# A hybrid network on one core: the selective-scan layers with another split of their work over the engines

## The chip, the cores and the metric

The kernel runs on one core of a Trainium2 chip. A core has five engines with instruction queues of their own: TensorE (PE, matrix products into PSUM), VectorE (DVE), ScalarE (ACT), GpSimd (POOL) and SyncE (SP, which here issues the DMAs). They meet only at semaphores. The metric is the device time of one execution in microseconds; lower is better.

## The reference, cut to what matters

The network takes x of shape (2, 16, 16, 64): two batches of 256 positions with 64 channels. It runs an edge-attention block, a rope attention, a wide attention, a mixture of experts, six selective-scan (mamba) layers and a last mixture of experts. Only the six layers, and what is loaded for them, are changed:

```python
# for each of the 6 layers, on h of shape (2, 256, 64); dI = 128, DS = 16 states, rank 16
r = h * rsqrt(mean(h * h, -1) + eps) * norm_w
u, z = split(r @ in_w, 2)                      # 128 channels each
uc = silu(causal_conv(u, cw, 4 taps) + cb)
dt_r, Bm, Cm = split(uc @ xp_w, (16, 16, 16))
dt = softplus(dt_r @ dt_w + dt_b)
# scan over the 256 positions, for each channel and each of the 16 states:
#   s[t] = exp(dt[t] * A) * s[t-1] + dt[t] * uc[t] * Bm[t];   y[t] = sum over states of s[t] * Cm[t]
h = h + ((y + uc * D) * silu(z)) @ out_w
```

## The kernel before, in words

A layer runs as two units, one for each batch, so there are 12 units (`UNITS`). A unit holds its 128 channels on the partitions and its 256 positions on the columns. The 16 states are done in four groups of four (`NSG`, `SG`), each group one tile of 128x1024. For each group the kernel needs a decay tile (`da`, four exponentials on ACT, L1405), a drive tile (`dbu`, dt times uc times B), one scan on DVE (L1133, 128x1024), the product of the states with C (`hc`), and the sum over states, which TensorE does by adding the four slices of `hc` into PSUM with four products by the identity matrix (`sum_y`, L664).

B and C are 16 rows each, and must stand on all 128 partitions. That is done in two ways. The f32 rows go to DRAM (`spill`) and come back broadcast (groups 1 to 3 of B and group 1 of C). Or the rows are split in three bf16 parts, stacked on 96 partitions (`stack`), and TensorE spreads one row at a time with a column of picks (`spread_b` L634, `spread_c` L643). DVE takes the tiles that TensorE spread (drive of group 0 at L1121, C products of groups 0, 2 and 3 at L1140). POOL takes those that came by DMA (drives of groups 1 to 3 at L1611, C product of group 1 at L1619).

While a unit is scanned, the next one is prepared: squares and mean on ACT and POOL, two transposes (`prep_transpose`), the input products with the convolution folded in (`prep_in`), tanh on ACT, `prep_uc` on DVE (L1078), the product that gives B, C and the rank-16 rows (`prep_x`, L623), the product for dt (`prep_dt` on PE, L627), and softplus as a polynomial in four quadratics (ACT L1391, POOL, DVE L1098 and L1102). After the last sum of a unit, DVE multiplies it by the gate (`gate`, L1085), TensorE projects it out (L672) and DVE adds it to the residual (L1089).

The order on each engine is written out by hand: `pe_step`, `v_step`, `a_step` and `p_step`, with eight units inside a loop of two turns. An engine works strictly in that order. In `pe_step` three products that nobody reads stand behind the first spread of C (`keep_awake`, L655). Weights come layer by layer into two tiles (`wmt`).

What an instruction of the loop waits for is a count of a semaphore: `m_y` is raised by the last sum of a unit, `m_gate` by the gate, `m_h` by each scan, `m_uc`, `m_xds`, `m_dt` by the pieces named so.

Of the kernel before, what the change touches and what calls it, by code (L numbers as in the profile page):

```python
# [13 lines left out]
F32 = mybir.dt.float32  # L14
# [5 lines left out]
P = 128  # L20
# [56 lines left out]
def hybrid(nc, x, const, w0, w1, w2, w3, w5, wm, rows, out):  # L77
    ctx = ExitStack()
    with ctx:
# [3 lines left out]
        spill = nc.dram_tensor("spill", (B, DS + SG, N), F32, kind="Internal").ap()  # L83
# [12 lines left out]
        wmt = [sb(f"wmt{k}", [P, WM.size]) for k in range(2)]  # L96
# [14 lines left out]
        pick_b = sb("pick_b", [P, 32], BF16)  # L111
# [88 lines left out]
        xds, stack = two("xds", [P, N]), two("stack", [P, N], BF16)  # L200
        rest = sb("rest", [64, N])
        wcv, alog, amat = two("wcv", [P, 2 * P]), two("alog", [P, DS]), two("amat", [P, DS])
        dmat = two("dmat", [P, P])
# [1554 lines left out]
```

## Time and profile before

| | us |
|---|---|
| median of 3 runs | 411.38 |
| the three runs | 409.92, 411.38, 411.42 |
| span of the profiled execution | 409.9 |
| the lowest run, the nearest to that span | 409.92 |
| busy: PE 340.5, DVE 314.7, ACT 249.1, POOL 210.6 | |
| first gate (unit 0) to last gate (unit 11) | 178.5 to 379.7 |

Busy shares are 83% for PE, 77% for DVE, 61% for ACT and 51% for POOL, over stages with different limits. The 12 units take the span from about 145 to 380 us. A row of the chain of waits is a piece of the work that ended last, followed back; a row of a timeline has start, duration, engine and line, operation, tiles written and read, the count of instructions merged in it, and in brackets the idle time ahead of it with who ended it. An f32 product is two instructions of TensorE, so "x24" at L664 is twelve products.

### The profile page before, as it was taken

Reading aid. Unit: us, or ns where it says so; the run is one execution under the profiler, and the core shown is the slowest. Engines: PE = TensorE matmul, PEld = TensorE weight load, DVE = VectorE, ACT = ScalarE, POOL = GpSimd, SP = SyncE. Lnnn points to the kernel's source line nnn. Section 1 sums busy time; section 2 is a strip of 40 time slices with the busy share of each in tenths; the row PEclk is TensorE's granted clock in tenths of the full one; section 3 lists DMA queues with packets and bytes.
Section 4 is the critical chain, followed back from the end, with each engine's and each line's share of the span. In section 5 each row is a group of like instructions: output and inputs, shape, how many; then the busy total and the mean of one; then the engine's idle time right before and its main releaser. Section 6 shows DMA issues by size and latency. Waiting matters only on the chain.

```text
span 409.9 us, 5884 instructions
## 1 busy us (share of the span) xinstructions
PE 340.5 (83%) x1818; PEld 235.1 (57%) x1818; DVE 314.7 (77%) x538; ACT 249.1 (61%) x681; POOL 210.6 (51%) x235
## 2 busy tenths in 40 slices
PE   5868998999899986888887979888888879768674
PEld 3356765565584654566664757566566647557442
DVE  2674678898653618779999799979988999998653
ACT  2012378888727455948778586948676786862170
POOL 1985000000000028788889698868977797882000
PEclk9985999999979997899999899899989999987868
DMA  7900000000002105142450515161342326050000
GB/s 238 403 7 1 2 1 2 0 2 2 0 2 64 40 4 206 44 165 75 173 178 31 208 43 205 29 220 62 144 162 86 123 86 210 3 203 0 2 0 13
DMA packets 11345, 35.24 MB, mean 86 GB/s; under 512 B 2368, under 2 KB 2992, under 8 KB 11192
## 3 DMA queue, kind: packets, MB, share of 16 engines
q1 hardware_dynamic: 11032, 34.61, 23.9%
q10 hardware_dynamic: 288, 0.33, 0.3%
q8 instruction: 12, 0.20, 0.2%
q14 instruction: 13, 0.11, 0.1%
HBM read 34.54 MB, written 0.39 MB: 85 GB/s over the span
## 4 chain that ended last, share of the span: by engine, by line
PE 53%; DVE 24%; ACT 12%; issue 5%; DMA 3%; POOL 2%; DVEq 0%; SPq 0%; POOLq 0%; ACTq 0%
PE PS L664 15%; DVE big L1133 7%; ACT PS L1405 4%; PE PS L511 4%; PE PS L643 3%; DVE big L1121 3%; DVE big L1140 3%; PE PS L475 2%; ACT sg L1368 2%; PE PS L289 2%; PE PS L295 2%; PE PS L627 2%; PE PS L405 2%; PE PS L575 2%; PE PS L485 2%
## 5 line engine op out<-in xcount | busy, mean ns | idle before, releaser
L1133 DVE TENSOR_TENSOR_SCAN big<-PS,big 128x1024 f32<-128x1024 f32 x48 | 109.3, 2284 | 3.0 <-ACT PS L1405 2.7
L664 PE MATMUL PS<-big,cst 128*128 128x256 f32 x384 | 96.0, 407 | 0.0
L1405 ACT ACTIVATE PS<-dt,amat 128x255 f32<-128x255 f32 x192 | 80.1, 466 | 25.4 <-DVE dt L1105 21.5
L1611 POOL TENSOR_TENSOR big<-dtu,big 128x1024 f32<-128x1024 f32 x36 | 84.2, 2356 | 7.2 <-DVE dtu L1108 6.6
L664 PEld LDWEIGHTS PS<-big,cst 128*128 128x128 f32 x384 | 76.8, 205 | 14.9 <-issue 3.7
L1644 POOL TENSOR_SCALAR lnv<-mv 128x4 f32<-128x4 f32 x1 | 0.4, 418 | 93.9 <-DVE mv L770 93.9
L1140 DVE TENSOR_TENSOR big<-big,PS 128x1024 f32<-128x1024 f32 x36 | 43.8, 1216 | 0.9
L1239 ACT ACTIVATE big<-PS 128x512 f32<-128x512 f32 (+1 forms) x43 | 24.8, 584 | 22.3 <-PE PS L511 7.3
L643 PE MATMUL PS<-stack,pick_b 96*128 96x256 bf16 x144 | 23.9, 292 | 17.0 <-DVE big L1140 9.2
L1286 ACT ACTIVATE big<-PS,big 128x256 f32<-128x256 f32 x64 | 29.8, 475 | 1.5 <-DVE big L902 1.5
L1619 POOL TENSOR_TENSOR big<-big 128x1024 f32<-128x1024 f32 x12 | 28.3, 2358 | 1.1 <-DVE big L1133 1.1
L643 PEld LDWEIGHTS PS<-stack,pick_b 96*128 96x128 bf16 x144 | 11.8, 102 | 27.0 <-DVE big L1140 12.5
L902 DVE TENSOR_REDUCE big<-PS 128x2 f32<-128x512 f32 x32 | 22.0, 688 | 6.5 <-PE PS L405 3.1
L655 PE MATMUL PS<-cst 128*128 128x256 f32 x102 | 26.2, 396 | 0.0
L511 PE MATMUL PS<-cst,big 128*128 128x128 f32 x128 | 20.9, 285 | 3.2 <-ACT big L1239 1.9
L1597 POOL TENSOR_TENSOR big<-big,quad_t 128x256 f32<-128x256 f32 x24 | 14.2, 612 | 15.5 <-ACT big L1391 15.5
L511 PEld LDWEIGHTS PS<-cst,big 128*128 128x128 f32 x128 | 13.5, 140 | 14.4 <-DVE big L911 6.9
L655 PEld LDWEIGHTS PS<-cst 128*128 128x128 f32 x102 | 19.0, 198 | 3.0 <-issue 0.7
L911 DVE TENSOR_SCALAR big<-big 128x256 f32<-128x256 f32 x64 | 19.7, 350 | 1.1
L1391 ACT ACTIVATE big<-PS,quad_t 128x256 f32<-128x256 f32 x48 | 18.9, 477 | 0.4
L295 PE MATMUL PS<-cst 128*128 128x256 f32 x62 | 18.7, 436 | 0.0
L1361 ACT ACTIVATE ht<-PS,wmt 64x256 f32<-64x256 f32 x24 | 11.3, 471 | 12.1 <-PE PS L609 11.8
(309 smaller groups left out, 624.6 us busy)
## 6 DMA issues: line engine op xcount, KB each, us to landing
big<-spill SPq DMA_DIRECT2D x48, 512.0 KB, 5.6
wmt<-in_wm SPq DMA_DIRECT2D x6, 418.0 KB, 3.2
w3t<-in_w SPq DMA_DIRECT2D x1, 1588.0 KB, 13.5
big<-routed SPq DMA_DIRECT2D x8, 128.0 KB, 3.0
w2t<-in_w SPq DMA_DIRECT2D x1, 896.0 KB, 10.1
cst<-in_const SPq DMA_DIRECT2D x1, 848.0 KB, 8.0
w5t<-in_w SPq DMA_DIRECT2D x1, 812.0 KB, 15.0
w1t<-in_w SPq DMA_DIRECT2D x1, 385.0 KB, 8.4
```

What stands on the lines that cost most here:

```text
L295: pe.matmul(PS[:, bank, N:2 * N], ident, CONST.of(cst, "rope")[:, 0:N], start=True, stop=True)
L511: last = pe.transpose(PS[:, 6 + t, m * N + a * P:m * N + (a + 1) * P], probs[:, i % SLOTS, a, m * P:(m + 1) * P], ident)
L643: last = pe.matmul(PS[:, 4 + c, s * N:(s + 1) * N], pick_b[0:96, col:col + 1].to_broadcast([96, P]), stack[b][0:96], start=True, stop=True)
L655: pe.matmul(idle_ps, ident, CONST.of(cst, "rope")[:, 0:N], start=True, stop=True)
L664: last = pe.matmul(yps, ident, hc[:, g, s], start=False, stop=(g == NSG - 1 and s == SG - 1))
L1133: v.tensor_tensor_scan(flat(hst[g][:]), flat(da[g % 2]), flat(dbu[:, g]), 0.0, ALU.mult, ALU.add).then_inc(sem("m_h"), 1)
L1140: v.tensor_tensor(hc[:, g], hst[g][:], BCv, ALU.mult).then_inc(sem("m_hc"), 1)
L1239: copy = lambda dst, src, **kw: act.activation(dst, src, ACT.Copy, **kw)
L1286: act.activation(probs[:, i % SLOTS, a], PS[:, i % 4, a * N:(a + 1) * N], ACT.Exp, bias=rowmax[:, i, a:a + 1], accum_out=rowsum[:, i, a:a ...
L1405: one = act.activation(da[g % 2][:, n, 1:N], dt[b][:, 1:N], ACT.Exp, scale=amat[k][:, col:col + 1])
L1611: pool.tensor_tensor(dbu[:, g], dtu[b][:].unsqueeze(1).to_broadcast([P, SG, N]), bsp[b][:, SG * (g - 1):SG * g], ALU.mult).then_inc(sem("m ...
L1619: pool.tensor_tensor(hc[:, 1], hst[1][:], csp[b][:], ALU.mult).then_inc(sem("m_hc_pool"), 1)
```

## The change

The arithmetic is the same network in another split:

- All weights of the six layers are loaded at the start (`wr`, `wxd`, `wout`, `cols`, `inz`, `wcv`, `winu`), and the rank-16 weight is multiplied into one 128x128 weight for dt (`wdt`), by transposes and products placed in the first attention stage. The loop over units is straight code for all 12.
- The biases of the convolution and of dt are rows of ones times a bf16 stack (`bias`), one more product each in `prep_in` and `prep_x`.
- The three bf16 parts of B and C are made inside PSUM: `prep_x` writes three copies of the rows (times two), ACT takes the first part out, TensorE subtracts it from the other two (`split_hi`), ACT takes the second out, TensorE subtracts it (`split_mid`), ACT takes the third.
- DVE now drives groups 0 and 1 and multiplies C only for group 3 (`weigh_last`, in two halves). POOL drives groups 2 and 3 and multiplies C for groups 0, 1 and 2. C of groups 0 to 2 and B of groups 2 and 3 come by DMA: five broadcasts of 512 KB a unit in place of four.
- The normed rows are written twice by ACT (`prep_hs`) in place of once by POOL. The residual is a product by the identity that starts the sum of the output projection, and ACT copies it back.
- Softplus is another formula: Abs, Exp, Tanh and three Squares on ACT, then two fused operations on DVE; POOL has no part in it.
- `keep_awake` stands only ahead of unit 0. `prep_uc` moves on DVE from behind scan 2 to behind scan 1. On TensorE the sums of group 0 move behind `prep_x` and `split_hi`.

```diff
--- before.py
+++ after.py
+            def prep_in(u):
+
+                i, b = divmod(u, 2)
+                pe.wait_ge(sem("m_ht"), u + 1)
+                pe.matmul(ups, bias[:, i, :, 0], ones[:], start=True, stop=False)
+                pe.matmul(ups, wcv[:, i, 0], ht[b][:, 3:3 + N], start=False, stop=False)
+                pe.matmul(ups, wcv[:, i, 1], ht[b][:, 1:1 + N], start=False, stop=True).then_inc(sem("m_in"), 1)
+                pe.matmul(zps, inz[:, i], ht[b][0:64, 3:3 + N], start=True, stop=True).then_inc(sem("m_in"), 1)
...
+                pe.matmul(dtp, bias[:, i, :, 1], ones[:], start=True, stop=False)
+                pe.matmul(dtp, wdt[:, i], uc[b], start=False, stop=True)
+                pe.matmul(xd[64:96], wxd[:, i, 0:32], uc[b], start=True, stop=True).then_inc(sem("m_xd"), 1)
+                pe.matmul(xd[0:64], wxd[:, i, 0:64], uc[b], start=True, stop=False).then_inc(sem("m_xd"), 1)
+
+            def split_hi(u):
+
+                pe.wait_ge(sem("m_xs"), 4 * u + 2)
+                pe.wait_ge(sem("m_sp"), 6 * u + 1)
+                pe.matmul(xd[0:32], less_hi[64:96], stack[u % 2][64:96], start=False, stop=False)
+                pe.matmul(xd[32:64], less_hi[64:96], stack[u % 2][64:96], start=False, stop=True).then_inc(sem("m_less"), 1)
+
+            def split_mid(u):
+
+                pe.wait_ge(sem("m_xs"), 4 * u + 3)
+                pe.matmul(xd[0:32], less_mid[32:64], stack[u % 2][32:64], start=False, stop=True).then_inc(sem("m_less"), 1)
...
+            def out_proj(u):
+
+                i, b = divmod(u, 2)
+                if u + 1 < UNITS:
+                    pe.wait_ge(sem("m_dt"), u + 2)
+                if u >= 2:
+                    pe.wait_ge(sem("m_ycp"), u - 1)
+                pe.matmul(hidp, ident, Y[:, :, b], start=True, stop=False)
                 pe.wait_ge(sem("m_gate"), u + 1)
                 for a in range(HALF):
-                    last = pe.matmul(hidp[:, a], yg[b][:, a * P:(a + 1) * P], WM.of(wmt[k], "out"),
-                                     start=True, stop=True)
...
-                if not first:
-                    sum_y(u + -1, nb, NSG - 1)
-                spread_b(u, b)
-                if not first:
-                    out_proj(u + -1, pk, nb)
-                pe.wait_ge(sem("m_dbu0"), u + 1)
-                spread_c(u, b, 0)
-                if not last:
-                    keep_awake(3)
-                sum_skip(u, k, b)
-                if not last:
-                    prep_transpose(u + 1, nk, nb)
-                pe.wait_ge(sem("m_hc"), u * 3 + 1)
-                spread_c(u, b, 2)
-                if not last:
-                    prep_in(u + 1, nk, nb, i * 2 + (s + 1) // 2 + 1)
-                sum_y(u, b, 0)
-                if not last:
-                    prep_x(u + 1, nk, nb)
-                if not last:
-                    prep_dt(u + 1, nk, nb)
-                pe.wait_ge(sem("m_hc"), u * 3 + 2)
-                spread_c(u, b, 3)
-                sum_y(u, b, 2)
-                sum_y(u, b, 1)
...
+            for u in range(UNITS):
+                more = u + 1 < UNITS
+                if u:
+                    sum_y(u - 1, 2)
+                    sum_last(u - 1)
+                spread_first(u)
+                if u:
+                    out_proj(u - 1)
+                spread_second(u)
+                if more:
+                    prep_transpose(u + 1)
+                    prep_in(u + 1)
+                spread_last(u)
+                if more:
+                    prep_x(u + 1)
+                sum_skip(u, u + 1 if more else None)
+                if more:
+                    split_hi(u + 1)
+                sum_y(u, 0)
+                if more:
+                    split_mid(u + 1)
+                sum_y(u, 1)
+            sum_y(UNITS - 1, 2)
+            sum_last(UNITS - 1)
...
+            for u in range(UNITS):
+                prep_dt(u)
+                if u:
+                    gate(u - 1)
+                drive(u, 0)
+                scan(u, 0)
+                drive(u, 1)
+                scan(u, 1)
+                if u + 1 < UNITS:
+                    prep_uc(u + 1)
+                scan(u, 2)
+                scan(u, 3)
+                weigh_last(u)
             scaled = hs2[0][:].rearrange("p a (b e) -> p a b e", b=B)
...
+            def prep_xd(u):
+
+                act.wait_ge(sem("m_xd"), 2 * u + 2)
+                act.activation(xds[u % 2][:], xd[64:96], ACT.Copy, scale=0.5).then_inc(sem("m_xs"), 1)
+                act.activation(stack[u % 2][64:96], xd[64:96], ACT.Copy, scale=0.5).then_inc(sem("m_xs"), 1)
+
+            def prep_softplus(u):
+
+                act.activation(sp_a, dtp, ACT.Abs).then_inc(sem("m_sp"), 1)
+                act.wait_ge(sem("m_sp"), 6 * u + 1)
+                act.activation(sp_u, sp_a, ACT.Exp, scale=-1.0).then_inc(sem("m_sp"), 1)
+                act.activation(sp_v, sp_a, ACT.Tanh, scale=0.5, bias=turn_t).then_inc(sem("m_sp"), 1)
+                act.wait_ge(sem("m_less"), 2 * u + 1)
+                act.activation(stack[u % 2][32:64], xd[32:64], ACT.Copy, scale=0.5).then_inc(sem("m_xs"), 1)
+                act.wait_ge(sem("m_sp"), 6 * u + 3)
+                act.activation(sp_3, sp_u, ACT.Square, bias=a2_t).then_inc(sem("m_sp"), 1)
+                act.activation(sp_1, sp_v, ACT.Square, bias=a_t).then_inc(sem("m_sp"), 1)
+                act.wait_ge(sem("m_less"), 2 * u + 2)
+                act.activation(stack[u % 2][0:32], xd[0:32], ACT.Copy, scale=0.5).then_inc(sem("m_xs"), 1)
+                act.wait_ge(sem("m_sp"), 6 * u + 5)
+                act.activation(sp_2, sp_1, ACT.Square, scale=LOG_ROOT, bias=b_t).then_inc(sem("m_sp"), 1)
+
...
+            for u in range(UNITS):
+                more = u + 1 < UNITS
+                drive(u, 2)
+                if more:
+                    prep_rms(u + 1)
+                drive(u, 3)
+                for g in range(3):
+                    weigh(u, g)
+                if more:
+                    prep_gz(u + 1)
 
...
```

Engine TensorE, the second half of a unit, from the product on the fresh uc to the first spread of the next unit. Before (L623 is `prep_x`, L627 `prep_dt`, L643 the spread of C for group 3, L664 the sums, L634 the spread of B):

```order
L664 MATMUL PS<-big,cst 128x256 x4
L623 MATMUL PS<-uc,wmt 112x256
L627 MATMUL PS<-xds,wmt 128x256
L643 MATMUL PS<-stack,pick_b 128x256 x4
L664 MATMUL PS<-big,cst 128x256 x12
L634 MATMUL PS<-stack,pick_b 128x256 x4
```

Now (L637 to L640 are `prep_x`, L685 `sum_skip`, L646 and L647 `split_hi`, L652 `split_mid`, L691 and L698 the sums, L659 the spread):

```order
L637 MATMUL PS<-ones,bias 128x256
L638 MATMUL PS<-unit_t,wdt 128x256
L639 MATMUL PS<-unit_t,wxd 32x256
L640 MATMUL PS<-unit_t,wxd 64x256
L685 MATMUL PS<-unit_t,w0t 128x256
L646 MATMUL PS<-stack,less_hi 32x256
L647 MATMUL PS<-stack,less_hi 32x256
L691 MATMUL PS<-big,cst 128x256 x4
L652 MATMUL PS<-stack,less_mid 32x256
L691 MATMUL PS<-big,cst 128x256 x8
L698 MATMUL PS<-big,cst 128x256 x4
L659 MATMUL PS<-stack,pick_b 128x256 x4
```

The four sums of group 0, which stood ahead of `prep_x`, now stand behind it and behind `split_hi`; all 16 sums follow in one piece.

Engine TensorE, the first half of a unit, from the output projection to `prep_x`. Before (L655 is `keep_awake`):

```order
L672 MATMUL PS<-wmt,yg 128x64 x2
L643 MATMUL PS<-stack,pick_b 128x256 x4
L655 MATMUL PS<-cst 128x256 x3
L650 MATMUL PS<-uc,dmat 128x256
L609 MATMUL PS<-cst,hs 128x128 x2
L643 MATMUL PS<-stack,pick_b 128x256 x4
L615 MATMUL PS<-ht,wcv 128x256
L616 MATMUL PS<-ht,wcv 128x256
L617 MATMUL PS<-ht,wmt 128x256
L664 MATMUL PS<-big,cst 128x256 x4
```

Now:

```order
L708 MATMUL PS<-Y,cst 128x128
L711 MATMUL PS<-wout,unit_t 128x64 x2
L659 MATMUL PS<-stack,pick_b 128x256 x4
L621 MATMUL PS<-cst,hs 128x128 x2
L628 MATMUL PS<-ones,bias 128x256
L629 MATMUL PS<-ht,w2t 128x256
L630 MATMUL PS<-ht,w2t 128x256
L631 MATMUL PS<-ht,inz 128x256
L659 MATMUL PS<-stack,pick_b 128x256 x4
```

The three idle products, the skip product and four sums have gone from this stretch; small bias and identity products have come.

Engine DVE, one unit from its gate on. Before (L1121 drive, L1133 scan, L1140 C product, L1078 uc, L1098 and L1102 the polynomial):

```order
L1085 TENSOR_TENSOR yg<-PS,gz 128x256
L1121 TENSOR_TENSOR big<-dtu,PS 128x1024
L1089 TENSOR_TENSOR Y<-Y,PS 128x2x64
L1133 SCALAR_TENSOR_TENSOR big<-PS,big 128x1024
L1140 TENSOR_TENSOR big<-big,PS 128x1024
L1133 SCALAR_TENSOR_TENSOR big<-PS,big 128x1024 x2
L1078 SCALAR_TENSOR_TENSOR uc<-PS,wmt,sg 128x256
L1140 TENSOR_TENSOR big<-big,PS 128x1024
L1133 SCALAR_TENSOR_TENSOR big<-PS,big 128x1024
L1140 TENSOR_TENSOR big<-big,PS 128x1024
L1098 SCALAR_TENSOR_TENSOR PS<-big,PS 128x256 x2
```

Now (L1130 gate, L1137 drive, L1146 scan, L1110 uc, L1156 C product, L1116 and L1119 the polynomial):

```order
L1130 TENSOR_TENSOR unit_t<-PS,unit_t 128x256
L1137 TENSOR_TENSOR big<-unit_t,PS 128x1024
L1146 SCALAR_TENSOR_TENSOR big<-PS,big 128x1024
L1137 TENSOR_TENSOR big<-unit_t,PS 128x1024
L1146 SCALAR_TENSOR_TENSOR big<-PS,big 128x1024
L1110 SCALAR_TENSOR_TENSOR unit_t<-unit_t,PS 128x256
L1146 SCALAR_TENSOR_TENSOR big<-PS,big 128x1024 x2
L1156 TENSOR_TENSOR big<-big,PS 128x512 x2
L1116 SCALAR_TENSOR_TENSOR big<-big 128x256
L1119 SCALAR_TENSOR_TENSOR big<-big 128x256
```

Between the gate and uc there stand two drives and two scans, where there were one drive, three scans and one C product.

## Rows read from the trace of the kernel before

**Rows 1.** Page: the chain by engine, and the broadcasts (count, size, us to landing).

```profile
PE 53%; DVE 24%; ACT 12%; issue 5%; DMA 3%; POOL 2%; DVEq 0%; SPq 0%; POOLq 0%; ACTq 0%
...
big<-spill SPq DMA_DIRECT2D x48, 512.0 KB, 5.6
```

**Rows 2.** Stretches, two neighbouring units: us, busy (instructions) by engine, PE clock, DMA.

```profile
271.60:289.40 17.80, 15.06 (x72) 10.93 (x72) 17.32 (x17) 13.33 (x38) 13.96 (x17) 1.00 0.34 118
289.40:309.00 19.60, 16.95 (x72) 12.11 (x72) 16.80 (x16) 13.75 (x38) 16.93 (x14) 0.91 0.35 132
```

**Rows 3.** Chain of waits in those units: start us, us, what.

```profile
283.71 5.18 PE PS L664 x24
288.89 0.45 PE PS L634 x4
289.37 1.22 DVE big L1121
290.71 2.30 DVE big L1133
...
301.73 6.80 PE PS L664 x24
```

**Rows 4.** Timeline of DVE, same unit; columns as told under time and profile.

```profile
285.96 0.89 DVE L1098 SCALAR_TENSOR_TENSOR PS<-big,PS 128x256 f32<-128x256 f32 x2
287.48 0.42 DVE L1105 TENSOR_TENSOR dt<-PS,sp_m 128x256 f32<-128x256 f32 x1
288.93 0.42 DVE L1085 TENSOR_TENSOR yg<-PS,gz 128x256 f32<-128x256 f32 x1
293.04 1.22 DVE L1140 TENSOR_TENSOR big<-big,PS 128x1024 f32<-128x1024 f32 x1
294.17 4.67 DVE L1133 TENSOR_TENSOR_SCAN big<-PS,big 128x1024 f32<-128x1024 f32 x2
298.75 0.46 DVE L1078 SCALAR_TENSOR_TENSOR uc<-PS,wmt,sg 128x256 f32<-128x256 f32 x1
```

**Rows 5.** Timeline of PE: prep_x.

```profile
299.27 0.69 PE L623 MATMUL PS<-uc,wmt 128*112 128x256 f32 x2 [0.65 <-DVE uc L1078]
```

**Rows 6.** Timeline of ACT behind the decays of group 3.

```profile
300.00 0.38 ACT L1377 ACTIVATE xds<-PS 112x256 f32<-112x256 f32 x1
300.41 0.42 ACT L1379 ACTIVATE stack<-xds 96x256 bf16<-96x256 f32 x1
301.16 0.45 ACT L1385 ACTIVATE PS<-PS,wmt 128x256 f32<-128x256 f32 x1 [0.34 <-PE PS L627]
```

**Rows 7.** Timeline of POOL: one drive.

```profile
289.35 2.35 POOL L1611 TENSOR_TENSOR big<-dtu,big 128x1024 f32<-128x1024 f32 x1
```

**Rows 8.** Stretches inside unit 289.4 to 309.0, and one of the last unit.

```profile
290.70:296.60 5.90, 4.99 (x24) 3.17 (x24) 5.77 (x5) 4.77 (x14) 5.74 (x6) 1.00 0.01 3
296.60:301.40 4.80, 3.68 (x17) 2.31 (x17) 4.80 (x4) 4.26 (x12) 4.80 (x4) 1.00 0.02 4
301.50:304.80 3.30, 3.30 (x10) 2.65 (x9) 3.11 (x4) 2.64 (x8) 1.92 (x4) 0.50 0.55 174
366.40:373.10 6.70, 4.45 (x12) 3.00 (x12) 6.63 (x5) 4.36 (x9) 5.35 (x3) 0.50 0.00 0
```

**Rows 9.** Timeline of unit 0: ACT and DVE.

```profile
149.78 0.48 DVE L1078 SCALAR_TENSOR_TENSOR uc<-PS,wmt,sg 128x256 f32<-128x256 f32 x1 [4.32 <-ACT zs L1371]
152.21 0.45 ACT L1385 ACTIVATE PS<-PS,wmt 128x256 f32<-128x256 f32 x1 [0.34 <-PE PS L627]
156.50 0.42 DVE L1105 TENSOR_TENSOR dt<-PS,sp_m 128x256 f32<-128x256 f32 x1
```

**Rows 10.** Timeline of DVE: gates of units 0, 10 and 11.

```profile
178.47 0.42 DVE L1085 TENSOR_TENSOR yg<-PS,gz 128x256 f32<-128x256 f32 x1 [1.70 <-PE PS L664]
...
362.85 0.42 DVE L1085 TENSOR_TENSOR yg<-PS,gz 128x256 f32<-128x256 f32 x1 [0.55 <-PE PS L664]
...
379.74 0.42 DVE L1085 TENSOR_TENSOR yg<-PS,gz 128x256 f32<-128x256 f32 x1 [1.77 <-issue]
```

More of the change, by code:

```diff
@@ L198, in hybrid @@
+        uc, gz, dt, dtu, yg, tu, zs, zt = ([unit_t[:, N * (2 * n + t):N * (2 * n + t + 1)] for t in range(2)]
+                                           for n in range(8))
         ht = two("ht", [P, N + 4])
         hs2 = two("hs2", [P, HALF, P])
[L200 to L203, printed above, removed]
+        xds, stack = two("xds", [32, N]), two("stack", [96, N], BF16)
@@ L708, in _, with keep_awake @@
-            keep_awake(7)
-            prep_transpose(0, 0, 0)
+            def keep_awake(count, bank=5):
+                for _ in range(count):
+                    pe.matmul(PS[:, bank, N:2 * N], ident, CONST.of(cst, "rope")[:, 0:N], start=True, stop=True)
+            keep_awake(7, 6)
+            prep_transpose(0)
             keep_awake(1)
-            prep_in(0, 0, 0, 1)
-            keep_awake(4)
-            prep_x(0, 0, 0)
+            pe.wait_ge(sem("m_weights"), 5)
+            prep_in(0)
@@ L714, in _ @@
+            keep_awake(3)
+            prep_x(0)
             keep_awake(1)
-            prep_dt(0, 0, 0)
+            split_hi(0)
+            keep_awake(1)
+            split_mid(0)
             keep_awake(5)
-            pe_step(0, 0, first=True)
-            with pe.Fori(0, 2) as i:
-                for s in range(1, 5):
-                    pe_step(i, s)
-            for s in range(9, 12):
-                pe_step(0, s, last=(s == 11))
-            sum_y(UNITS - 1, 1, NSG - 1)
-            out_proj(UNITS - 1, 1, 1)
+            for u in range(UNITS):
[20 more added lines that the diff above has]
+                sum_y(u, 1)
@@ L1142, in _, with drive @@
-            prep_uc(0, 0, 0)
-            v_step(0, 0, first=True)
-            with v.Fori(0, 2) as i:
-                for s in range(1, 5):
-                    v_step(i, s)
-            for s in range(9, 12):
-                v_step(0, s, last=(s == 11))
+                v.tensor_tensor(yg[u % 2], yps, gz[u % 2], ALU.mult).then_inc(sem("m_gate"), 1)
+            def drive(u, g):
+                v.wait_ge(sem("m_BC"), 3 * u + g + 1)
+                if g == 0:
+                    v.wait_ge(sem("m_dtu"), u + 1)
+                v.tensor_tensor(dbu[:, g], dtu[u % 2].unsqueeze(1).to_broadcast([P, SG, N]), BCv, ALU.mult)\
+                    .then_inc(sem("m_dbu"), 1)
```

626 lines of the change are left out of this document (284 added, 342 removed).

## The prediction

> **What bounds the kernel now.** I read the page's chain first: TensorE holds 53% of what ended last and DVE 24% [rows 1]. Then I cut the 12 units into stretches. They come in two lengths, 17.8 us with the PE clock at its upper level (1.00, 2.4 GHz) and 19.6 us with a mean of 0.91 [rows 2]. In the short unit DVE is busy for 17.32 us of 17.8, and yet the chain does not stay on it: it runs over the twelve sums on PE, 5.18 us (0.43 each), the spread of B, the first drive and the scan [rows 3]. So two cycles are nearly equal, the work of DVE and a loop that goes through DVE, PE and ACT. In the long unit the same twelve sums take 6.80 us [rows 3], because the clock is at 0.50 (1.2 GHz) from 301.5 to 304.8 [rows 8], and 1.62 us arrive at the gate. A change gains only if it shortens both cycles.
>
> **DVE, part by part.** From one gate to the next it will do: gate 0.44 (288.93 to 289.37), two drives with their handover at 1.34 (289.37 to 290.71) [rows 3, 4], four scans at 2.3, uc 0.46, the last C product in two halves, about 1.25 (one was 1.22), and four small operations at 0.46 where five stood [rows 4]. That is 0.44 + 2.68 + 9.2 + 0.46 + 1.25 + 1.84 = 15.9 us in place of 17.3. By DVE alone a unit would fall from a mean of 18.4 ((362.85 - 178.47) / 10 [rows 10]) to about 16.2.
>
> **POOL and DMA.** POOL does five tiles of 2.35 us [rows 7] and small work of under 2 us, 13.5 us a unit. The drives are ready before their scans and the C products before their sums, except at the very end (below). Five broadcasts replace four; each lands in about 5.6 us [rows 1], and the first is wanted about 5 us after the rows leave ACT. If it is late by a microsecond the delay goes into POOL's wait for the squares of the next unit. Cost taken: nothing; without that cover, up to 1 us a unit.
>
> **The loop through PE, which I expect to decide.** The new order puts all sixteen sums behind prep_x and split_hi, and these behind uc. I follow it from the start of a gate:
> - Gate 0.44, first drive 1.34, scan 0 until the next operation 2.33 (290.71 to 293.04), second drive 1.34, scan 1 2.29 (half of 294.17 to 298.75): 7.74 us to uc [rows 3, 4].
> - uc to the first product behind it: 0.52 (298.75 to 299.27) [rows 4, 5].
> - prep_x was one f32 product, 0.69 with its tail. It gets two more at 0.43 and a bf16 one at 0.11 (four bf16 spreads took 0.45 [rows 3]): 1.66, and 0.04 to ACT. 1.70.
> - ACT copies the rows twice, 0.41 and 0.38 between starts, and takes Abs, 0.45 [rows 6], with 0.04 for the handover: 1.28. The skip product (0.43) lies beside this.
> - split_hi 0.22, sixteen sums 6.91, split_mid 0.11 between the first four and the rest, some 0.15 for three small weights: 7.4 us, and the next gate starts.
>
> The sum is 7.74 + 0.52 + 1.70 + 1.28 + 7.4 = 18.6 us at full clock. The same steps for the kernel before (0.44, 1.34, 2.33, 1.13, 4.58, 0.52, 0.73, 0.43, 0.63, 0.54, 5.22) give 17.9 where 17.8 was measured, so the method is good to a few tenths. DVE will be done 2.4 us before the last sum and wait at its gate. What was won by moving uc ahead of a scan (2.3 us) goes back through four more sums behind uc (1.7) and two more products in prep_x (1.0).
>
> ACT's work hides: two more small copies and no sigmoid copy for u; from Abs to the last Square six operations of about 0.4 and a wait for split_mid, some 3.5 us. They end about 4 us ahead of the last sum.
>
> **The clock.** Between gate and uc, 7.7 us, PE now has the projection (0.9 with the identity product), two spreads (1.2), two transposes (0.45) and prep_in (1.6): 4.1 us busy, 53%. Before, the stretch 290.7 to 296.6 was busy for 4.99 of 5.9 us, thanks to the three keep_awake products and the skip; 296.6 to 301.4 was busy for 3.68 of 4.8, and after it the clock fell for 3.3 us. In the last unit, which has no such products, it was at 0.50 from 366.4 to 373.1 [rows 8]. So I expect a fall in every unit, not in every second. One fall costs 1.62 us where it lies on sums, less where it lies on the thin stretch. Bounds: 0 if all of it hides, 3.2 if two falls lie on the path. I take 1.1, nearer the one fall measured, since it begins in the thin part and then covers prep_x and the first sums. The unit becomes 19.7 us.
>
> The Trainium skill (TensorE: Matmul & The Clock Gate, section Why this matters for your kernels) warns only of long idle gaps between bursts of matmuls. By that rule the clock would hold here; that is the second rival below. The trace disagrees: PE never stood still for long between 296.6 and 301.4, and the clock fell [rows 8].
>
> **Unit 0 and the ends.** For unit 0, uc needs only tanh and no longer the copies of z: up to 1.4 us sooner than 149.78. But three keep_awake products and the longer prep_x stand in PE's queue, so Abs comes perhaps 0.4 sooner than 152.21, and dt about 0.5 sooner than 156.50 [rows 9]. From dt to gate 0 there were 178.47 - 156.50 = 22.0 us [rows 9, 10]. Now: dt and dtu 0.92, then 7.3 to uc, 10.9 to the gate, and 1.1 for the clock, 20.2. Together -2.3. Gates 0 to 10: ten units of 19.7 against 184.4, +12.6. Gate 10 to gate 11 was 16.9 us [rows 10]: now POOL is last there, scan 2 ends 10.0 after the gate, its C product at 12.5, eight sums 3.5, and a clock that is low for part of it, 17.4: +0.5. The residual copy moves from DVE to ACT at the end, +0.1. The loads, casts and products for the weights stand in the stages from 10 to 60 us, where POOL and ACT idle for microseconds and DMA is at rest: nothing, at most 1.
>
> Sum: -2.3 + 12.6 + 0.5 + 0.1 = +10.9. On the profiled execution, 409.9, that is 420.8. The median of the runs shown is 1.5 above it, and I count from there: 411.4 + 10.9 = 422.3, say 422.5.
>
> **The rivals.**
> - Forecast: the loop through PE, 18.6 and about one fall a unit, 416 to 430. Chance 0.50.
> - The clock costs more. A low clock also stretches prep_in, whose tanh has only about 1 us in hand before uc, and prep_x (1.7 us longer at 1.2 GHz). With 2 to 3 us a unit: 432 to 442. For it: the last unit before stayed low for 6.7 us. Against: sixteen sums in one piece are the densest stretch of the kernel, and the clock rose in such a piece before. Chance 0.20.
> - The clock holds or falls only in the thin stretch: 18.6 a unit, so 12 x 1.1 = 13 less than the forecast, 409.5 to 413, no change that can be told. Chance 0.15.
> - Faster: DVE is the bound. A unit takes 16.2, ten units 162 against 184.4, and the time is about 388. It decides if the last sum is there when dtu is ready, which is 16 us after the gate. For it: DVE loses 1.4 us and was busy for 17.32 of 17.8. Against: the sums would have to start 2.4 us sooner, and the order gives them no way past split_hi, which waits for ACT, which waits for prep_x. Chance 0.10.
> - A step I price at nothing does not hide (a broadcast that keeps POOL, fetching of the long straight code): slower still, 425 to 440. Chance 0.05.
>
> About 0.5% (2 us) is what a measurement of this kernel can tell from no change. Faster 0.10; same 0.15; slower 0.75. The range of 8 in 10 runs from 410, where the clock holds, to 438; the forecast's own is 416 to 430.
>
> **What would show it.** Right: gates 19 to 20.5 us apart; DVE idle for 2 to 4 us ahead of each gate with the sums as its releaser; DVE busy for under 16 us a unit; a PE clock at 0.50 in every unit; the sixteen sums starting about 3.6 us after uc. Wrong: gates 16 to 17 us apart and DVE above 95% busy would mean that the sums are not on the path; gates at 18.6 with a clock of 1.00 would leave the clock term at nothing; a wait of DVE at uc for tanh, or of POOL for a broadcast, would mean another loop is longer than this one.

## The result and the profile after

The change made the kernel slower: 461.62 us (median of 4 runs, 458.55 to 463.82) against 410.69 us on the same chip (409.92 to 411.42), a ratio of 1.123 with a 95% interval of 1.117 to 1.129. The forecast was 422.5 with a range of 410 to 438: the direction was right, the size was not. The profiled execution has a span of 461.8 us (before: 409.9), so 51.9 us are to be found. It is one of the two longer ones of the four (463.58 and 463.82 us; the others took 458.55 and 459.67), which matters for the second loss below.

The page of the changed kernel, its chain by engine and its broadcasts (they answer to [rows 1]), and the PE clock in tenths for 40 slices:

```profile
PEclk9965699799969995958795979597858876887977
...
PE 67%; ACT 13%; DVE 11%; POOL 4%; issue 4%; DMA 1%; DVEq 0%; POOLq 0%; SPq 0%; ACTq 0%
...
big<-spill SPq DMA_DIRECT2D x60, 512.0 KB, 6.1
```

The chain has moved to TensorE, from 53 to 67%, and most slices of the loop (from the 17th on) show a clock under 9 tenths. Gates 0, 10 and 11 in the timeline of DVE (to [rows 10]), and dt of unit 0 (to [rows 9]):

```profile
170.55 0.42 DVE L1121 SCALAR_TENSOR_TENSOR unit_t<-PS,big 128x256 f32<-128x256 f32 x1
...
194.13 0.42 DVE L1130 TENSOR_TENSOR unit_t<-PS,unit_t 128x256 f32<-128x256 f32 x1 [2.76 <-PE PS L698]
...
416.39 0.42 DVE L1130 TENSOR_TENSOR unit_t<-PS,unit_t 128x256 f32<-128x256 f32 x1 [2.77 <-PE PS L698]
...
432.47 0.42 DVE L1130 TENSOR_TENSOR unit_t<-PS,unit_t 128x256 f32<-128x256 f32 x1 [2.25 <-issue]
```

That gives the ledger, in us of the two profiled executions:

| stretch | before | after | difference | forecast |
|---|---|---|---|---|
| start to dt of unit 0 | 156.50 | 170.55 | +14.05 | -0.5 |
| dt to gate 0 | 21.97 | 23.58 | +1.6 | -1.8 |
| gates 0 to 10 (10 units) | 184.38 | 222.26 | +37.9 | +12.6 |
| gate 10 to gate 11 | 16.89 | 16.08 | -0.8 | +0.5 |
| gate 11 to the end | 30.2 | 29.3 | -0.8 | +0.1 |

So there are two losses. The first is in the loop. Two neighbouring units as stretches (to [rows 2]), and the first of them cut into four (to [rows 8]); columns: us, busy (instructions) of PE, PEld, DVE, ACT, POOL, PE clock, DMA share, GB/s:

```profile
283.20:288.20 5.00, 2.24 (x16) 1.47 (x14) 4.92 (x4) 3.63 (x13) 3.12 (x3) 0.88 0.43 174
288.20:296.80 8.60, 8.48 (x20) 3.80 (x20) 8.26 (x7) 5.10 (x14) 7.14 (x4) 0.50 0.00 0
296.80:300.00 3.20, 3.00 (x8) 2.31 (x9) 0.88 (x2) 2.15 (x6) 0.00 (x0) 0.50 0.51 137
300.00:306.50 6.50, 6.50 (x30) 5.13 (x29) 1.74 (x3) 3.16 (x8) 3.13 (x2) 0.95 0.89 340
sum 23.30, PE 20.22 PEld 12.72 DVE 15.79 ACT 14.03 POOL 13.39; mean PE 5.06 PEld 3.18 DVE 3.95 ACT 3.51 POOL 3.35
...
306.60:327.60 21.00, 17.38 (x73) 11.29 (x71) 15.74 (x14) 14.04 (x39) 13.40 (x8) 0.84 0.31 99
```

Long units (23.3 to 23.5 us) and short ones (21.1) take turns. DVE is busy for 15.79 us in a unit (forecast 15.9). In the long unit PE did 2.24 us of work in the first 5.0, and then ran at 0.50 (1.2 GHz) for some 13 us; in the short one for about 7. The timeline of PE in the long unit shows what lay under the low clock (to [rows 3, 5]):

```profile
283.71 0.66 PE L711 MATMUL PS<-wout,unit_t 128*128 128x64 f32 x4
284.95 0.61 PE L659 MATMUL PS<-stack,pick_b 96*128 96x256 bf16 x4 [0.58 <-DVE big L1137]
286.69 0.46 PE L621 MATMUL PS<-cst,hs 128*128 128x128 f32 x2 [1.12 <-ACT hs L1391]
288.31 0.40 PE L628 MATMUL PS<-ones,bias 96*128 96x256 bf16 x1 [1.17 <-ACT ht L1401]
288.50 1.06 PE L629 MATMUL PS<-ht,w2t 128*128 128x256 f32 x2
...
292.33 0.42 PE L637 MATMUL PS<-ones,bias 96*128 96x256 bf16 x1
...
297.00 0.37 PE L646 MATMUL PS<-stack,less_hi 32*32 32x256 bf16 x1 [0.21 <-ACT big L1431]
...
297.32 3.61 PE L691 MATMUL PS<-big,cst 128*128 128x256 f32 x8
300.86 0.28 PE L652 MATMUL PS<-stack,less_mid 32*32 32x256 bf16 x1
301.07 3.72 PE L691 MATMUL PS<-big,cst 128*128 128x256 f32 x16
```

Read in it three waits, 0.58, 1.12 and 1.17 us, and then prep_in from 288.31, prep_x from 292.33 and the first four sums (eight records, 3.61 us; at full clock eight take 1.9) all at half speed.

The second loss stands ahead of the loop. Timelines of DVE and of POOL in the second layer norm:

```profile
37.43 3.12 DVE L818 TENSOR_TENSOR X<-X,mv 128x256 f32<-128x256 f32 x1
40.59 1.57 DVE L820 TENSOR_TENSOR X<-X,rowt 128x256 f32<-128x256 f32 x1
42.19 1.57 DVE L808 TENSOR_TENSOR X<-X,rstd 128x256 f32<-128x256 f32 x1
43.79 3.19 DVE L824 TENSOR_TENSOR X<-X,rowt 128x256 f32<-128x256 f32 x1
```

```profile
37.18 3.09 POOL L1592 TENSOR_TENSOR unit_t<-big,bias 96x1536 f32<-96x1536 f32 x1
40.34 3.14 POOL L1595 CAST bias<-unit_t 32x1536 bf16<-32x1536 f32 x2
43.56 3.14 POOL L1597 TENSOR_TENSOR unit_t<-unit_t,bias 32x1536 f32<-32x1536 f32 x1
46.76 1.54 POOL L1599 CAST bias<-unit_t 32x1536 bf16<-32x1536 f32 x1
```

The same four operations of DVE took 0.42 or 0.43 each before. Now three of them end some 0.3 us behind an instruction of POOL (40.55 behind 40.27, 43.76 behind 43.48, 46.98 behind 46.70); the other ends at 42.16, in the middle of the row of two casts. The Trainium skill has the rule that I had not weighed: GPSIMD Engine Reference, the Specifications, says that the SBUF interfaces are shared with VectorE and contend "with DVE instructions in a 2-port perf mode or with two SBUF inputs". The trace agrees: an operation of 0.42 us took up to 3.2 here.

A part of the second loss is not the change's at all. Four edited kernels of the next section have the changed kernel's instructions ahead of the loop, and so two groups can be told: `dt` of unit 0 came at 170.55 in the changed kernel and at 170.88 in e1, but at 167.16, 167.55 and 167.94 in e8, e10 and e11. Between e11 and the changed kernel the difference arises in one place, a fall of the clock between 83 and 90 us. The same products there, changed kernel first, then e11:

```profile
83.64 2.07 PE L415 MATMUL PS<-big 32*128 32x256 f32 x8
...
83.51 1.13 PE L415 MATMUL PS<-big 32*128 32x256 f32 x8
```

There the clock is 0.57 in the one and 1.00 in the other. That costs some 2.6 us, so of the +14.05 about 11 stand in the traces of all five kernels, and the rest in some.

### The profile page after: what moved, and what is told of

It is laid out like the page before. It is cut to its first block, busy times and chain, and to the rows that moved or that the text cites. A ratio compares the mean times of both kernels' runs of the same rounds, so it can differ in the third digit from the quotient of the medians.

```text
span 461.8 us, 5567 instructions
## 1 busy us (share of the span) xinstructions
PE 378.7 (82%) x1822; PEld 246.1 (53%) x1822; DVE 309.6 (67%) x514; ACT 256.4 (56%) x701; POOL 206.2 (45%) x162
## 4 chain that ended last, share of the span: by engine, by line
PE 67%; ACT 13%; DVE 11%; POOL 4%; issue 4%; DMA 1%; DVEq 0%; POOLq 0%; SPq 0%; ACTq 0%
PE PS L691 17%; PE PS L698 4%; PE PS L521 4%; PE PS L659 4%; PE PS L631 3%; PE PS L639 2%; ACT ht L1401 2%; PE PS L291 2%; PE PS L629 2%; PE PS L638 2%; PE PS L630 2%; PE PS L640 2%; PE PS L485 2%; PE PS L415 2%; PE PS L297 2%
## 5 line engine op out<-in xcount | busy, mean ns | idle before, releaser
L1146 DVE TENSOR_TENSOR_SCAN big<-PS,big 128x1024 f32<-128x1024 f32 x48 | 109.7, 2290 | 1.7 <-ACT PS L1453 0.3
L1646 POOL TENSOR_TENSOR big<-big 128x1024 f32<-128x1024 f32 x36 | 84.5, 2350 | 11.4 <-issue 5.8
L1453 ACT ACTIVATE PS<-unit_t,amat 128x255 f32<-128x255 f32 x192 | 81.7, 468 | 5.5 <-DVE big L1146 2.8
L691 PE MATMUL PS<-big,cst 128*128 128x256 f32 x288 | 78.6, 429 | 0.0
L691 PEld LDWEIGHTS PS<-big,cst 128*128 128x128 f32 x288 | 59.6, 214 | 12.5 <-issue 1.1
L1637 POOL TENSOR_TENSOR big<-unit_t,big 128x1024 f32<-128x1024 f32 x24 | 57.5, 2400 | 5.0 <-issue 3.3
L1628 POOL TENSOR_TENSOR unit_t<-unit_t 128x256 f32<-128x256 f32 x12 | 8.7, 725 | 73.1 <-ACT unit_t L1421 73.1
L659 PE MATMUL PS<-stack,pick_b 96*128 96x256 bf16 x144 | 27.0, 320 | 11.0 <-DVE big L1137 11.0
L1137 DVE TENSOR_TENSOR big<-unit_t,PS 128x1024 f32<-128x1024 f32 x24 | 29.0, 1208 | 0.3
L1130 DVE TENSOR_TENSOR unit_t<-PS,unit_t 128x256 f32<-128x256 f32 x12 | 5.1, 425 | 32.7 <-PE PS L698 30.4
L659 PEld LDWEIGHTS PS<-stack,pick_b 96*128 96x128 bf16 x144 | 13.6, 108 | 24.0 <-DVE big L1137 13.1
L698 PE MATMUL PS<-big,cst 128*128 128x256 f32 x96 | 22.7, 379 | 0.0
L1377 ACT ACTIVATE sqs<-PS 128x64 f32<-128x64 f32 x20 | 4.3, 219 | 31.6 <-PE PS L711 31.6
L1119 DVE SCALAR_TENSOR_TENSOR big<-big 128x256 f32<-128x256 f32 x12 | 5.1, 426 | 22.4 <-ACT big L1443 22.4
L698 PEld LDWEIGHTS PS<-big,cst 128*128 128x128 f32 x96 | 18.2, 190 | 2.5
```

The source lines that it names most:

```text
L659: last = pe.matmul(PS[:, 4 + c, s * N:(s + 1) * N], pick_b[:, col:col + 1].to_broadcast([96, P]), stack[u % 2][:], start=True, stop=True)
L691: pe.matmul(yps, ident, hc[:, g, s], start=False, stop=False)
L698: last = pe.matmul(yps, ident, hc[:, NSG - 1, s], start=False, stop=(s == SG - 1))
L1137: v.tensor_tensor(dbu[:, g], dtu[u % 2].unsqueeze(1).to_broadcast([P, SG, N]), BCv, ALU.mult)\
L1146: v.tensor_tensor_scan(flat(hst[:, g]), flat(da[g % 2]), flat(dbu[:, g]), 0.0, ALU.mult, ALU.add).then_inc(sem("m_h"), 1)
L1453: one = act.activation(da[g % 2][:, n, 1:N], dt[u % 2][:, 1:N], ACT.Exp, scale=amat[:, u // 2, col:col + 1])
```

## The experiments

Theory A: PE's clock falls because the stretch between a gate and prep_x has little work, and that is most of the 38 us of the loop. Theory P: POOL's new work for the weights holds up DVE ahead of the loop, some 10 us (the expectations call each of the two "Theory A" in its own run). Rivals, called B there: the new order is long by itself (sixteen sums behind uc); or the late start comes from PE's added transposes and products. Two marks measure the part ahead of the loop: the first exponentials of the attention on ACT (49.43 us before, 59.67 after), and `hs`, the normed rows that open unit 0 (144.43 and 158.89). The edits are in the changed kernel unless said otherwise. The medians of "before" on the chips used lay at 410.7 to 412.2 us.

### e1: products in the thin stretch

```diff
+ keep_awake(2, 6)     # behind out_proj(u - 1)
  spread_second(u)
+ keep_awake(2, 6)
  prep_transpose(u + 1)
+ keep_awake(3, 6)
  prep_in(u + 1)
+ keep_awake(2, 5)     # ahead of spread_last(u), behind that spread's own wait
```

> The changed kernel with seven to twelve products of 128x256 more in the thin stretch of TensorE's list in each unit: two behind out_proj, two behind the second spread, three between the transposes and prep_in (all into the free half of bank 6), two ahead of the last spread (bank 5). Nothing else is changed. Theory A (the clock falls in the thin stretch of nearly every unit, and that is where the gates lost some 38 us): the granted clock of units 0 to 10 goes from about 0.78 to over 0.93, the long units of 23.4 us and the short ones of 21.1 us both become 18.5 to 19.5 us, and the time falls by 30 to 40 us, to 422 to 432 us. Rival B (the loop is long by its chain of waits, whatever the clock): units stay at 21 to 23 us or grow by the 1 to 2 us of the added products, 460 to 475 us.

Measured: 432.62 us (430.25 to 435.51), ratio to before 1.054 (1.041 to 1.067). All units became 19.23 us, with a clock of 0.99 over the loop. The time is 29 us shorter, though nine products a unit were added: rival B is out. But 19.2 is 0.8 more than the 18.4 of before.

### e2: POOL's weight work behind the layer norms

```diff
+ pool.wait_ge(sem("r_qm"), 4)
  pool.wait_ge(sem("ld_brow"), 48)
```

> The changed kernel with GpSimd's splitting of the bias columns and its other preparation of the Mamba weights held back behind the masking of the attention's queries, so that none of it runs beside the layer norms at 36 to 50 us. Nothing is left out. Theory A (VectorE's operations with two SBUF inputs wait there for GpSimd's whole instruction): the operations of lines 808 to 824 take 0.42 us again instead of 1.6 to 3.2, the first attention exponentials come at about 50 us instead of 59.7, and the time falls by 8 to 11 us, to 451 to 454 us. Rival B (the start is late because of the transposes and products for the weights on TensorE and of the clock that is low there): the time falls by under 3 us.

Measured: 463.58 us (459.36 to 464.58), no gain at all. The first half of the forecast held: the four operations took 0.42 again and the first exponentials came at 51.00. Then it was given back. DVE and PE of e2 some microseconds later:

```profile
52.37 3.79 DVE L942 TENSOR_SCALAR big<-big 128x256 f32<-128x256 f32 x2
...
56.87 3.98 DVE L942 TENSOR_SCALAR big<-big 128x256 f32<-128x256 f32 x2
```

```profile
56.22 1.10 PE L521 MATMUL PS<-cst,big 128*128 128x128 f32 x4 [2.75 <-DVE big L942]
```

Two divisions take 0.62 us where POOL is at rest; the four pairs between 52 and 68 us took 12.2 us together instead of 2.5. They have one tensor in SBUF as input (and a column of scalars), and still wait beside POOL: the collision had only been moved to the attention. By its time alone this run would have killed theory P; the timeline shows that it had moved the cause, not removed it. hs of unit 0 came at 158.21, where the changed kernel had 158.89.

### e3: both edits

> The changed kernel with both edits, the products in the thin stretch and GpSimd's weight work behind the layer norms. If both theories hold and the two losses are independent: 462 - 38 - 10 = 414 us, within 5 us of the kernel before. If the gain of the prologue is given back at the weights' readiness for the first unit, about 424 us.

Measured: 433.95 us (433.61 to 434.32): e1's gain, and nothing from e2's edit, as e2 alone says. Both forecasts, 414 and 424, missed.

### e4: the kernel before without its three products

```diff
- if not last:
-     keep_awake(3)
```

> The kernel before without its keep_awake(3) in each step of the loop, nothing else. Theory A: these three products are what holds the clock in the loop before; without them the clock falls once in each unit or in every other, as in the changed kernel, and the eleven units get 1.5 to 3.5 us longer each: 427 to 448 us. Rival B (the order of the list matters, with 12 sums between the spreads, and the three products do not): 409 to 413 us.

Measured: 430.33 us (428.67 to 432.37), ratio 1.052 (1.040 to 1.064). Two neighbouring units:

```profile
258.10:279.00 20.90, 17.84 (x68) 12.14 (x67) 17.03 (x16) 13.59 (x38) 15.32 (x16) 0.76 0.27 92
279.00:299.80 20.80, 17.74 (x68) 12.19 (x67) 17.60 (x17) 13.69 (x40) 15.67 (x16) 0.75 0.37 122
```

Ten units take 203.7 us instead of 184.4: +1.9 a unit. Three products a unit that nobody reads were worth 18 to 19 us in the kernel before; the change took them out.

### e5: POOL's and DVE's work where the other rests

```diff
- pool.wait_ge(sem("ld_brow"), 48)      # and the six operations of the split
+ pool.wait_ge(sem("ln_norm"), 6)       # weights only, behind the expert stage's norms
...
  v.tensor_copy(wT, PS[0:NE, 3]).then_inc(sem("x_wTs"), 1)
+ v.wait_ge(sem("ld_brow"), 48)         # the split, on DVE: six operations
```

> The changed kernel with the weight work moved out of the layer norms and the attention: GpSimd forms the convolution's and D's weights (5.3 us) behind the second layer norm of the expert stage (at about 130 us), and the three-way split of the bias rows (six operations of up to 96x1536) is done by VectorE at about 142 us, where it waits 6.8 us for the routed rows. Nothing is left out. Theory A (in e2 the loss only moved: GpSimd then ran at 50 to 68 us beside the attention, where two divisions of line 942 took 3.8 us instead of 0.62): the first hs of the loop comes at 145 to 148 us instead of 158.9, and the time falls by 10 to 13 us, to 449 to 452 us. Rival B (TensorE's added transposes and products for the weights, and the spares that are gone): under 3 us.

Measured: 453.62 us (451.13 to 455.22), 8.0 less than the changed kernel, 2 short of what was expected. hs of unit 0 came at 150.49, 8.4 sooner, but 6.1 later than before. Here too there are two groups: e6, e7, e9 and e15 have the same placement and had hs at 147.62 to 147.76, 3.2 later than before.

### e6 and e7: the order ahead of prep_x, with products added

e6 is e5 with e1's products and `sum_skip` right behind `prep_in(u + 1)`; e7 puts `sum_y(u, 0)` there too, and leaves out the two products ahead of the last spread.

> e5 with the added products of e1 in the thin stretch, and sum_skip (0.7 us) moved ahead of the last spread. If the losses are independent: 432.6 - 12 = 421 us from the first two, and up to 0.7 us a unit from the third if the sums behind prep_x set the gate: 413 to 421 us.

> e5 with seven added products a unit in the thin stretch, and the D product and the first four sums ahead of the last spread and of prep_x, so that 12 sums instead of 16 stand behind prep_x. In e1 those four sums waited from 279.8 (their input was there) to 284.0. If the chain prep_x, splits, 16 sums sets the gate: units of 17.2 to 18.2 us instead of 19.2, and 398 to 410 us, under the kernel before. If VectorE or ScalarE's chain to dt sets it instead (prep_x is 2 us later): units of 19 to 20 us and 418 to 428 us.

Measured: 436.68 us (436.27 to 438.51) and 442.60 us (439.93 to 446.31). Both missed. Units were 20.4 us in e6 and 20.3 in eight of e7's ten, at full clock, over e1's 19.2: what was put ahead of prep_x delays it, and with it the splits. In e7 PE stood for ACT's stacks, where e1 had sums to do (weight loads, PEld, show it):

```profile
279.71 0.09 PEld L647 LDWEIGHTS PS<-stack,less_hi 32*32 32x32 bf16 x1 [1.79 <-ACT stack L1444]
...
280.89 0.09 PEld L653 LDWEIGHTS PS<-stack,less_mid 32*32 32x32 bf16 x1 [1.07 <-ACT stack L1453]
```

These waits had a price of their own: in this unit of e7 and the next the clock fell at about the second of them (here 0.50 from 280.5 to 287.0), and the two took 23.3 and 21.9 us.

### e8: e7's order without added products

```diff
  prep_in(u + 1)
+ sum_skip(u, u + 1)
+ sum_y(u, 0)
  spread_last(u)
  prep_x(u + 1)
```

> The changed kernel with the D product and the first four sums ahead of the last spread and prep_x, nothing else: no product is added. Theory A (the clock falls because of idle time between the gate and prep_x): the stretch is denser by 2.7 us of products, part of the falls go, units of 19 to 21 us instead of 22.2, 425 to 450 us. Rival B (the order is the whole cause, not the clock): 418 to 428 us with units of 18.5 us. If neither: 455 us or more.

Measured: 480.65 us (478.55 to 483.88), the slowest of all; of the recorded outcomes only "if neither, 455 us or more" fits. Units of 24 us, the clock at 0.79 in each. The four sums moved forward did not hold the clock; they fell under it:

```profile
267.72 0.69 PE L621 MATMUL PS<-cst,hs 128*128 128x128 f32 x2 [1.12 <-ACT hs L1391]
269.45 0.40 PE L628 MATMUL PS<-ones,bias 96*128 96x256 bf16 x1 [1.04 <-ACT ht L1401]
...
274.25 3.62 PE L691 MATMUL PS<-big,cst 128*128 128x256 f32 x8
```

Against e7 (20.3) that is 3.7 us of clock a unit, and the rest is e7's longer chain. Here work that the kernel does anyway was moved ahead of prep_x, but behind the waits, and did not help; in e1, e10 and e11 added products that lie in the waits did. No run adds idle products behind the waits alone, so that it is their place and nothing else that counts is not shown.

### e9: the version built from these

e5's placement, seven products (e1's without the last two), and the splits one place later, so that PE sums while ACT makes the stacks:

```diff
  prep_x(u + 1)
  sum_skip(u, u + 1)
- split_hi(u + 1)
  sum_y(u, 0)
- split_mid(u + 1)
+ split_hi(u + 1)
  sum_y(u, 1)
+ split_mid(u + 1)
```

> The changed kernel with the weight work moved as in e5, seven added products a unit (two behind out_proj, two behind the second spread, three ahead of prep_in; the two ahead of the last spread of e1 are left out, which stood before prep_x for 0.45 us), and the splits one place later in TensorE's list: the first four sums between prep_x and the high split, the next four between the two splits, so that TensorE adds while ScalarE makes the stacks (in e1 it stood idle there 0.95 us a unit, in e7, where no sum stood there, 1.79 and 1.07). Theory: 432.6 - 8.4 - 11 x (0.45 + 0.95) = 409 us, units of 17.8 to 18.2 us; range 403 to 416. Rival (the stretch before prep_x is too thin again without the two products, the clock falls in some units): 418 to 430.

Measured in 12 runs: 409.67 us (408.23 to 413.39), ratio to before 0.999 (0.995 to 1.002), where 409 had been worked out. Units are 18.02 us:

```profile
272.70:290.70 18.00, 17.52 (x87) 12.44 (x85) 15.37 (x15) 14.06 (x39) 13.39 (x9) 1.00 0.42 147
```

It repairs the change, and does not beat the kernel before: ten units take 180.2 us instead of 184.4, and the start takes 2.8 of that back (dt of unit 0 at 159.31, before 156.50).

### e10 and e11: which wait has to be filled

e10 has only the three products between the transposes and prep_in, e11 only the four behind out_proj and the second spread, both in the changed kernel.

> The changed kernel with only the three products between the transposes and prep_in (0.65 us a unit, in TensorE's wait for ht), nothing else. If each hole counts by itself and this, the last before prep_x, is the one that matters: near e1, 430 to 440 us. If the clock answers to how much TensorE has done over the whole stretch, some of the falls stay: 440 to 455 us. If it does nothing: 460 us.

> The changed kernel with only the four products in the early part of the thin stretch (two behind out_proj, two behind the second spread, 0.87 us a unit). Read against e10: the same alternatives, 430 to 440 us, 440 to 455 us, or 460 us.

Measured: 431.12 us (430.08 to 431.86) and 425.94 us (424.08 to 427.89). Each does nearly all of it; e11 is better than any of its forecasts. In e10 most units are 18.8 us and three of ten are 19.8 to 19.9; in e11 all are 18.8:

```profile
266.90:285.70 18.80, 16.39 (x81) 11.43 (x80) 15.39 (x14) 14.08 (x39) 13.34 (x8) 1.00 0.41 141
```

e11 is the changed kernel at full clock, since its four products lie in waits: prep_in starts 5.10 us after the gate, where it was 5.07. Ten units take 188.3 us, so falls of the clock cost the changed kernel 222.3 - 188.3 = 34.0. The kernel before had falls too: six of its ten units take 17.8 us, four take more, and ten of 17.8 would be 178.1 in place of 184.4. At equal, full clock the new order is thus 10.2 us longer (1.0 a unit), and of the +37.9 the clock is 34.0 - 6.3 = 27.7.

### e12: POOL's work alone, in the kernel before

```diff
+ for n in range(5):   # each waits for the one before
+     pool.tensor_tensor(spin[:], w3t[0:96, 0:1536], w3t[0:96, 0:1536], ALU.mult)
```

> The kernel before with five products of 96x1536 by 96x1536 added on GpSimd behind the expert weights, at 35 to 52 us; their result is used by nobody. Nothing is left out. Theory A (VectorE's operations with two SBUF inputs wait for the whole instruction that GpSimd runs): lines 787 to 793 take 1.5 to 3.2 us instead of 0.42, the first attention exponentials come at 57 to 61 us instead of 49.4, and the time is 8 to 11 us longer, 419 to 422 us. Rival B (the late start of the changed kernel came from TensorE's weight work and clock): 411 to 413 us.

Measured: 423.60 us (418.11 to 424.76), ratio 1.025 (1.016 to 1.034). DVE and POOL:

```profile
38.60 2.85 DVE L790 TENSOR_TENSOR X<-X,rowt 128x256 f32<-128x256 f32 x1
41.48 2.85 DVE L778 TENSOR_TENSOR X<-X,rstd 128x256 f32<-128x256 f32 x1
44.37 2.85 DVE L794 TENSOR_TENSOR X<-X,rowt 128x256 f32<-128x256 f32 x1
```

```profile
35.54 14.28 POOL L1544 TENSOR_TENSOR spin<-w3t 96x1536 f32<-96x1536 f32 x5
```

14.28 / 5 = 2.86: each operation of DVE waits out one of POOL's. The first exponentials came at 59.99 (changed kernel 59.67) and dt of unit 0 at 167.92, 11.4 later than before. Work that nobody reads, on an engine off the path, gives 11.4 of the 14 us, which is what e11, without the fall at 83 us, has as well (167.94). A part of it comes by way of PE, which waits for DVE: its clock from 40 to 50 us was 0.62, and 0.90 before.

### e13 to e15: the last terms

e13 is e9 with `sum_skip` between the last spread and prep_x. e14 is e13 with the products for the dt weights moved behind the attention's projections. e15 is e9 without the seven products.

> e9 with sum_skip (0.7 us) between the last spread and prep_x instead of behind prep_x. In e9 TensorE stands idle there about 0.4 us, from the last spread's end at 298.08 to uc at 298.42, and sum_skip must wait for zs (298.0). prep_x would start some 0.3 us later, the chain behind it is 0.7 us shorter: 0.3 to 0.4 us a unit less, 405 to 407 us. Rival (what counts is when prep_x starts, as e6 hints, where sum_skip ahead of the last spread cost 1.1 us a unit): 411 to 415 us.

> e13 with the products of the two small weights for dt (12 records, 2.9 us, at 37.9 us) moved behind the projections of the first attention, ScalarE's copy of them behind the group norm's rate, and two spare products of 128x256 in their old place. If their place keeps the clock at half until 48 us (before: 42), the first exponentials come at 49 to 50 us instead of 52.3 and the time is 2 to 3 us under e13. If the clock there follows something else: within 1 us of e13.

> e9 without its seven added products a unit: the weight work moved, and the splits one place later. Theory A (holes between the gate and prep_x make the clock fall, the order is worth some 1 us a unit by itself): the clock falls in most units, 21 to 22.5 us each, 435 to 452 us. Rival B (the good order alone would have done it): units of 18 us, 407 to 415 us. Against e8 (24.0 us a unit): if A holds with e8 too, the clock falls here about as often as in e5, 40 to 50 per cent of the loop at half.

Measured: e13 409.42 us (407.23 to 411.90), ratio 0.999 (0.996 to 1.003); e14 410.31 us (407.24 to 412.70), ratio 1.000 (0.996 to 1.003); e15 435.59 us (433.91 to 436.15). In e13 units fell to 17.83, but its profiled run had hs of unit 0 at 150.37 where e9's had 147.65 (the same code; the clock from 70 to 80 us was 0.68 and 1.00); the medians do not tell them apart. 17.83 is also what a unit of the kernel before takes at full clock, so the best order found here is not shorter than that one; it has no falls. The 405 to 407 us expected of e13 were not reached. In e14 the first exponentials came 1.2 us sooner (49.97), and hs at the same time (150.50). e15's units are 20.5 to 20.6 at a clock of 0.83: the good order without the products costs 2.5 a unit, and its clock is low for less of the loop than e5's (0.77).

## Why the prediction was wrong

- **DVE's work**, 15.9 us a unit: right, 15.79. So were its wait at each gate (2.4; measured 2.77), POOL (13.5; 13.4), and that DVE would not be the bound (rival at 388).
- **The loop through PE at full clock**, 18.6: right. uc came 7.63 after the gate (forecast 7.74), and e11's units are 18.83. Of the signs named for "right", DVE's wait, its work and a clock of 0.50 in every unit held; the gates (21.1 to 23.5 us apart, not 19 to 20.5) and the sums (6.4 us after uc in the long unit, not 3.6) did not.
- **The clock term**, 1.1 us a unit: this step failed. It is 22.23 - 18.83 = 3.4, 34 us in ten units, and outside my bounds of 0 to 3.2. I priced one fall at the 1.62 us that it had cost the twelve sums of the old order. What the runs put in its place is a longer fall: 13.7 and 6.8 us at half clock in alternate units, over prep_in, prep_x and, in the long unit, the first sums, which all lie on the path. In the long unit, from the start of its gate, prep_x starts after 9.09 us (e11: 7.79), split_hi after 13.76 (11.00), the middle split after 17.62 (13.14), the next gate after 23.31 (18.83). That is 1.3 + 1.5 + 1.7 = 4.5 us; the short unit loses 2.3. I had named the mechanism in the rival "the clock costs more", and gave it 2 to 3 us and a chance of 0.20. The nearer row was the last unit before, 6.7 us at 0.50 without the three products [rows 8]; e4 says that leaving these out costs 1.9 a unit even in the old order.
- **The rule of the Trainium skill** against which I argued (TensorE: Matmul & The Clock Gate, Why this matters for your kernels: no long idle gaps between bursts) would have held the clock. The trace disagrees again: the longest wait of PE between the gates of units 0 and 10 is 1.2 us, and the clock fell in each unit.
- **"The loads, casts and products for the weights ... nothing, at most 1"**: this step failed too, by 14 us. I asked if POOL was idle there, not what DVE did beside it. e12 makes 11.4 us of it with POOL's work alone, e5 takes 8.4 back. The other 2.6 are the fall of the clock from 83 to 90 us, which e11 does not have with the same code there. Why it comes in some runs stays open, and so do the 3.2 us that the start is still late with e5's placement (hs at 147.6 in e9, 144.43 before).
- **dt to gate 0**, 20.2: 23.58, with the clock at 0.50 for some 10 us over prep_in and prep_x, as in the loop; no run tests this stretch by itself. **hs to dt of unit 0**: 12.1 before and 11.7 after, the -0.5 that was forecast. Gate 10 to 11 (+0.5) and the end (+0.1) came out at -0.8 each.

With the measured 3.4 for the clock and 14 for the prologue the forecast's own sum gives 411.4 + 10.9 + 10 x 2.3 + 14.5 = 460: no third term of this size is missing.

## What to carry to other kernels

Before taking filler products out of a list, find the waits of PE that they stood in, and price their loss by a stretch that already lacks them: while the clock is low the products take nearly twice as long (eight sums 3.61 us in place of 1.89), and what that costs is set by how many of them lie on the path. An engine at rest is not free room: before giving POOL some microseconds of work, list what DVE runs beside it. And when moving a suspected cause changes nothing, look in the trace whether it has gone or only moved.

## What the runs showed of the hardware

- A 128x256 f32 operation of DVE with two inputs in SBUF waited for the end of the instruction that POOL was in: 0.42 us became 2.85 beside products of 2.86 (e12), 3.1 beside 3.1 (after). A pair of divisions with one tensor input in SBUF, f32, waited too: 0.62 became 3.8 to 4.0 (e2). The reductions from PSUM kept their 0.68 to 0.69.
- In the changed kernel the clock fell in every unit with no wait of PE over 1.2 us, and four products of about 0.5 us each in a unit's waits held it (from gate 0 to gate 11: 0.98 in e11, 0.77 after).
- Useful products moved behind the waits did not do what four idle ones in the waits did: 480.65 against 425.94 us (e8, e11).
- The same instructions had a fall of the clock in one profiled kernel and none in another: from 83 to 90 us it was 0.57 in the changed kernel and 1.00 in e11, which is worth 2.6 us.
